# Second block of a two-block transformer: the last token tile of each feed-forward is multiplied one turn later, and the first feed-forward products stand two a step over four steps

## What is computed

```
qkv = x @ qkv_w                      # 16 heads of 16
attn = softmax(where(node_mask, q @ k.T / 4, -inf)) @ v
attn_out = attn @ proj_w + proj_b
x = x + gate_msa * modulate(layernorm(attn_out), shift_msa, scale_msa)
mlp_out = gelu(x @ fc1_w + fc1_b) @ fc2_w + fc2_b
x = x + gate_mlp * modulate(layernorm(mlp_out), shift_mlp, scale_mlp)
```

## Time and profile before

| what | value |
|---|---|
| median of 3 runs | 1455.85 us |
| profiled execution: its time, its span | 1457.03 us, 1455.2 us |
| busy share of TensorE, VectorE, ScalarE, GpSimd | 90%, 55%, 53%, 52% |
| granted TensorE clock over the span | 0.978 |
| length of turn 12 | 63.75 us |

### The profile page before, as it was taken

One profiled execution on the slowest core, in us unless ns is written; L12 is line 12 of the kernel. 1 busy time (PEld: TensorE's weight loads), 2 busy tenths in 40 slices (PEclk: granted clock), 3 DMA queues, 4 the chain that ended last, 5 costly groups with the idle time before them and its releaser, 6 DMA issues. The chain is left out here.

```text
span 1455.2 us, 24552 instructions
## 1 busy us (share of the span) xinstructions
PE 1309.6 (90%) x8789; PEld 1004.0 (69%) x8789; DVE 803.2 (55%) x2240; ACT 770.5 (53%) x1262; POOL 757.1 (52%) x939
## 2 busy tenths in 40 slices
PE   4898999999999999999999997989888898988777
PEld 3676777777777777777777775666666666665556
DVE  3766645645646656656645643464655556454452
ACT  3565665665665765665655752544544353453522
POOL 3788876776776776776776761020413222140323
PEclk9999999999999999999999998999999999999988
DMA  8432222223213213213213215353424242433100
GB/s 258 130 127 57 71 84 72 73 75 83 74 64 89 75 58 88 78 55 88 79 54 110 92 41 164 113 152 108 151 67 145 61 155 93 123 116 86 45 2 29
DMA packets 98259, 133.98 MB, mean 92 GB/s; under 512 B 16802, under 2 KB 51498, under 8 KB 98130
## 3 DMA queue, kind: packets, MB, share of 16 engines
q1 hardware_dynamic: 96850, 131.80, 30.3%
q10 hardware_dynamic: 1280, 0.53, 0.2%
HBM read 72.64 MB, written 58.75 MB: 90 GB/s over the span
## 5 line engine op out<-in xcount | busy, mean ns | idle before, releaser
L617 POOL TENSOR_SCALAR shifted<-shifted,row_max 128x512 f32<-128x512 f32 x512 | 360.6, 719 | 220.1 <-DVE row_max L1380 218.2
L1380 DVE CUSTOM_DVE_ANT_0 shifted<-score,bias 128x512 f32<-128x512 f32 x512 | 332.7, 687 | 255.4 <-PE score L855 165.6
L1091 ACT ACTIVATE probs<-turned 128x512 f32<-128x512 f32 x512 | 278.2, 596 | 211.4 <-PE turned L867 209.8
L867 PE MATMUL turned<-ident,shifted 128*128 128x128 f32 x2048 | 270.0, 275 | 6.8 <-POOL shifted L617 6.0
L867 PEld LDWEIGHTS turned<-ident,shifted 128*128 128x128 f32 x2048 | 233.6, 141 | 55.6 <-issue 26.6
L783 PE MATMUL dense<-w_down,hidden 128*128 128x256 f32 x1024 | 253.3, 383 | 0.8 <-ACT hidden L1072 0.8
L610 POOL TENSOR_SCALAR bias<-dist,scale 128x1024 f32<-128x1024 f32 x192 | 220.0, 1146 | 13.6 <-DMA down_bias<-in_L_cond_b 13.6
L855 PE MATMUL score<-k_rows,q_rows 97*128 97x512 f32 x512 | 205.2, 456 | 22.1 <-DVE row_max L1380 10.1
L783 PEld LDWEIGHTS dense<-w_down,hidden 128*128 128x128 f32 x1024 | 185.6, 191 | 32.6 <-issue 9.6
L763 PE MATMUL dense<-feat_m,w_up 128*128 128x512 f32 x768 | 188.4, 400 | 3.5 <-ACT hidden L1072 1.8
L763 PEld LDWEIGHTS dense<-feat_m,w_up 128*128 128x128 f32 x768 | 144.3, 192 | 37.1 <-ACT hidden L1072 5.3
(11 more groups left out here) (138 smaller groups left out, 1497.3 us busy)
## 6 DMA issues: line engine op xcount, KB each, us to landing
qk_rows<-qk_high SPq DMA_DIRECT2D x128, 256.0 KB
q_rows<-qk_rows SPq DMA_DIRECT2D x64, 384.0 KB
qk_rows<-qk_low SPq DMA_DIRECT2D x64, 256.0 KB
k_rows<-qk_rows SPq DMA_DIRECT2D x68, 192.0 KB
x_in_t<-in_x SPq DMA_DIRECT2D x8, 512.0 KB, 3.8
x_res<-in_x SPq DMA_DIRECT2D x8, 512.0 KB, 5.5
x_mid<-x_norm SPq DMA_DIRECT2D x8, 512.0 KB, 3.3
x_in_t<-x_mid SPq DMA_DIRECT2D x8, 512.0 KB, 3.9
```

The costliest lines, as they stand in the source:

```text
L617: ins = pool.tensor_scalar(shifted[:, u % 3, i, :], shifted[:, u % 3, i, :], -1.0, row_max[:, t % 6:t % 6 + 1], ALU.mult, ALU.add)
L867: mm = pe.transpose(turned_bank[z % 2][:, HALF * kk + P * i:HALF * kk + P * i + P], shifted[:, u % 3, i, P * kt:P * kt + P], ident[:, :])
L1091: act.activation(probs[:, u % RING, 2 * pair:2 * pair + 2, :], turned_bank[z % 2][:, :].rearrange("p (a c) -> p a c", a=2), ACT.Exp)\
L1380: dve.tensor_tensor_reduce(shifted[:, u % 3, i, :], score_bank[t % 2], bias[:, u % 2, i, :], 1.0, 3.0e38, ALU.add, ALU.min, row_max[:, t % ...
```

## The change

In turns 9 to 15 a new table `HEADS` holds. Turn 8 keeps the old one under the name `ENTER`. The last token tile of the down product of pass n-1 isn't made in turn n any more but in turn n+1, at place 7, as the piece `late`, with its eight chunks in one run; `normalize` of that pass moves from step 0 to step 3 of turn n+1, and GpSimd's `inverse_std` and `norm_offset` move with it. `t2` moves from place 7 to 9 and `qk` 3 from 8 to 10. The eight `up` pieces stand at places 13, 16, 19 and 22, two at each, instead of four at 10 and four at 13. ScalarE takes them in two groups of four, at places 16 and 22 (`HEADS_GELU`). The remaining 24 down chunks stand at places 25 to 35. In step 2 VectorE does `peaks_of` before the four `add_tile`, and no longer after them. The end after turn 15 has a list `TAIL` of its own with the late tile between `wout` and `t2`.

```diff
@@ -64,14 +64,26 @@
 
 
 
-    HEADS = {0: [("v", 3), ("t3", 0), ("t3", 1)], 1: [("t1", 0), ("t1", 1)], 2: [("wout", 0), ("wout", 1)],
+
+    ENTER = {0: [("v", 3), ("t3", 0), ("t3", 1)], 1: [("t1", 0), ("t1", 1)], 2: [("wout", 0), ("wout", 1)],
              3: [("wout", 2), ("wout", 3), ("qk", 0)], 5: [("qk", 1)],
              6: [("qk", 2)], 7: [("t2", 0), ("t2", 1)], 8: [("qk", 3)],
              10: [("up", 0), ("up", 1), ("up", 2), ("up", 3)], 13: [("up", 4), ("up", 5), ("up", 6), ("up", 7)],
              19: [("down", 0)], 23: [("down", 1)], 28: [("down", 2)], 35: [("down", 3)]}
     HEAD_STEPS = H // 2 + 4
-    HEADS_DOWN = {16: (0, 4), 17: (4, 6), 19: (6, 9), 20: (9, 11), 22: (11, 14), 23: (14, 16), 25: (16, 19),
+    ENTER_DOWN = {16: (0, 4), 17: (4, 6), 19: (6, 9), 20: (9, 11), 22: (11, 14), 23: (14, 16), 25: (16, 19),
                   26: (19, 21), 28: (21, 24), 29: (24, 25), 31: (25, 28), 34: (28, 29), 35: (29, 32)}
+
+    HEADS = {0: [("v", 3), ("t3", 0), ("t3", 1)], 1: [("t1", 0), ("t1", 1)], 2: [("wout", 0), ("wout", 1)],
+             3: [("wout", 2), ("wout", 3)], 4: [("qk", 0)], 5: [("qk", 1)], 6: [("qk", 2)], 7: [("late", TT - 1)],
+             9: [("t2", 0), ("t2", 1)], 10: [("qk", 3)], 13: [("up", 0), ("up", 1)], 16: [("up", 2), ("up", 3)],
+             19: [("up", 4), ("up", 5)], 22: [("up", 6), ("up", 7)], 28: [("down", 0)], 31: [("down", 1)],
+             35: [("down", 2)]}
+    HEADS_DOWN = {25: (0, 6), 26: (6, 7), 28: (7, 12), 29: (12, 14), 31: (14, 19), 34: (19, 22), 35: (22, 24)}
+    LATE_AT = 7
+    TAIL = [("t3", 0), ("t3", 1), ("wout", 0), ("wout", 1), ("wout", 2), ("wout", 3), ("late", TT - 1), ("t2", 0),
+            ("t2", 1)] + [("up", c) for c in range(FCH)] + [("down", t) for t in range(TT)]
+    HEADS_GELU = {16: (13, 16), 22: (19, 22)}
 
     ANY = {0: [("v", 0), ("v", 1)], 1: [("t3", 0), ("t3", 1)], 2: [("v", 2), ("v", 3)], 3: [("t1", 0), ("t1", 1)],
            4: [("wout", 0)], 5: [("wout", 1)], 6: [("wout", 2)], 7: [("wout", 3)], 9: [("qk", 0)],
...
@@ -92,28 +104,35 @@
     def bias_by_act(u):
         return u % 4 == 3
 
-    def pass_of(piece, n):
+    def of_turn(piece, n):
+
+        if piece[0] == "late":
+            return (("down", piece[1]), n - 2) if n - 2 >= B else None
         m = n - 1 if piece[0] in BACK else n + 1 if piece[0] in FRONT else n
-        return m if 0 <= m < N else None
+        return (piece, m) if 0 <= m < N else None
+
+    def pieces(table, k, n):
+        found = [of_turn(p, n) for p in table.get(k, [])]
+        return [x for x in found if x is not None]
 
     def listed(table, n):
-        return [(p, pass_of(p, n)) for k in sorted(table) for p in table[k] if pass_of(p, n) is not None]
+        return [x for k in sorted(table) for x in pieces(table, k, n)]
+
+    def tail():
+        return [of_turn(p, N) for p in TAIL]
 
 
     PLACE = []
     for second in (HEADS, ANY):
         order = listed(FIRST, -1)
         for n in range(N):
-            order += listed(FIRST if n < B else second, n)
-        order += listed(second, N)
+            order += listed(FIRST if n < B else ENTER if n == B and second is HEADS else second, n)
+        order += tail() if second is HEADS else listed(second, N)
         PLACE.append({x: i for i, x in enumerate(order)})
     chosen = {"any": 0}
 
     def place(piece, n):
         return PLACE[chosen["any"]][piece, n]
-
-    def pieces(table, k, n):
-        return [(p, pass_of(p, n)) for p in table.get(k, []) if pass_of(p, n) is not None]
...
@@ -699,6 +718,9 @@
                 else:
                     add_shift(n - 1, 0)
                     inverse_std(n - 1, 0)
+                    if n - 2 >= B:
+                        inverse_std(n - 2, 1)
+                        norm_offset(n - 2)
 
                     piece_ready(pool, ("up", 0), n - 1)
                     add_shift(n - 1, 1)
@@ -707,9 +729,6 @@
                 if n + 1 < N:
                     mask(n + 1)
                     value_mask(n + 1)
-                if n > B:
-                    inverse_std(n - 1, 1)
-                    norm_offset(n - 1)
 
             def turn(n):
                 if short(n):
...
@@ -974,25 +995,28 @@
 
             def turn(n):
                 if short(n):
+                    table, down = (ENTER, ENTER_DOWN) if n == B else (HEADS, HEADS_DOWN)
                     for p in range(HEAD_STEPS):
                         attended = p >= 5 and p % 2 == 1
                         if 2 <= p < 2 + H // 2:
                             pair_scores_of(n, p - 2)
                         for k in range(3 * p, 3 * p + 2):
-                            for piece, m in pieces(HEADS, k, n):
+                            for piece, m in pieces(table, k, n):
                                 dense(piece, m)
-                            if k in HEADS_DOWN:
-                                down_chunks(n - 1, *HEADS_DOWN[k])
+                            if k in down:
+                                down_chunks(n - 1, *down[k])
+                            if k == LATE_AT and n - 2 >= B:
+                                down_chunks(n - 2, FCH * (TT - 1), FCH * TT)
                         if attended:
                             attend_heads(n, (p - 5) // 2)
                         if 2 <= p < 2 + H // 2:
                             turn_peaks(n, p - 2)
                         if 3 <= p < 3 + H // 2:
                             turned_scores_of(n, p - 3)
-                        for piece, m in pieces(HEADS, 3 * p + 2, n):
+                        for piece, m in pieces(table, 3 * p + 2, n):
                             dense(piece, m)
-                        if 3 * p + 2 in HEADS_DOWN:
-                            down_chunks(n - 1, *HEADS_DOWN[3 * p + 2])
+                        if 3 * p + 2 in down:
+                            down_chunks(n - 1, *down[3 * p + 2])
                         if attended:
                             heads_to_tokens(n, (p - 5) // 2)
                     return
...
@@ -1015,8 +1039,10 @@
                         to_tokens(n, gq)
 
             def epilogue():
-                for piece, m in listed(ANY if chosen["any"] else HEADS, N):
+                for piece, m in listed(ANY, N) if chosen["any"] else tail():
                     dense(piece, m)
+                    if piece[0] == "down" and m == N - 2:
...
@@ -1145,12 +1171,14 @@
 
             def turn(n):
                 if short(n):
+                    table, gelus = (ENTER, {}) if n == B else (HEADS, HEADS_GELU)
+                    later = [k for group in gelus.values() for k in group]
                     for p in range(HEAD_STEPS):
                         for k in range(3 * p, 3 * p + 2):
-                            for piece, m in pieces(HEADS, k, n):
-                                dense(piece, m)
-                        if p == 0 and n - 2 >= B:
-                            normalize(n - 2)
+
+                            for x in gelus.get(k, () if k in later else (k,)):
+                                for piece, m in pieces(table, x, n):
+                                    dense(piece, m)
                         if p >= 5 and p % 2 == 1:
                             take_heads_out(n, (p - 5) // 2)
                         if 2 <= p < 2 + H // 2:
@@ -1158,7 +1186,9 @@
                         if 3 <= p < 3 + H // 2:
                             for a in range(2):
                                 head_exp(n, 2 * (p - 3) + a)
-                        for piece, m in pieces(HEADS, 3 * p + 2, n):
+                        if p == 3 and n - 2 >= B:
+                            normalize(n - 2)
+                        for piece, m in pieces(table, 3 * p + 2, n):
                             dense(piece, m)
                         if n == B and p == 6:
                             take_high(w_out, raw_out[1], "wout_loaded", "out_high", 2)
@@ -1186,9 +1216,9 @@
                     take_high(w_up, raw_up[1], "wup_loaded", "up_high", 2)
 
             def epilogue():
-                for piece, m in listed(ANY if chosen["any"] else HEADS, N):
+                for piece, m in listed(ANY, N) if chosen["any"] else tail():
                     dense(piece, m)
-                    if piece == ("t3", DC - 1) and short(N - 1):
+                    if piece == ("t2", DC - 1) and short(N - 1):
                         normalize(N - 2)
 
             run(act, prologue, turn, epilogue)
...
@@ -1490,22 +1520,22 @@
 
             def turn(n):
                 if short(n):
+                    table = ENTER if n == B else HEADS
                     for p in range(HEAD_STEPS):
-                        for piece, m in pieces(HEADS, 3 * p, n):
+                        for piece, m in pieces(table, 3 * p, n):
                             dense(piece, m)
-                        if p == 2:
-                            if n == B:
-                                first_norm("norm", 1, n - 1)
-                            else:
```

(19 more changed lines are left out.)

## The result

The changed kernel takes 1468.67 us (median of 6 runs, 1463.77 to 1471.45), the kernel before 1455.59 in the same rounds. The ratio is 1.0079, 95% interval 1.0055 to 1.0103: slower, by 11.5 us by the ratio (the medians differ by 13.1). The profiled execution has a span of 1467.8 us against 1455.2.

The account below looks back on a forecast made before the run. TensorE bounds a turn: some 54 us of products, 7.6 of waits, plus clock loss. 63.8 + 1.0 + 3.8 - 4.1 + 1.8 + 1.0 = 67.3 us a turn; together +15.4 on 1457.0, median 1471 us, range 1449 to 1485.

Parts of the forecast that it names:

- case A: The sum as forecast: TensorE's waits change place and become longer, 1460 to 1483 us; chance 0.50.
- Steps 2 and 3: TensorE waits 2.5 us before the second pair's scores and 1.5 before the second turn_peaks; net +1.0 us a turn.
- The two groups of gelus: TensorE waits 1.9 us for ScalarE's gelus before up products in steps 4 and 7; +3.8 us a turn.
- What steps 4 to 11 and the edge give back: Shorter waits for split peaks, attend_heads and t3 in steps 4 to 11 and at the turn's edge; -4.1 us a turn.
- The transfers of peaks: Turned scores wait for transfers taking 4.7 us: 1.3 in step 4, 0.8 in step 6; +1.8 us net a turn.
- The clock: TensorE's clock falls in steps 2 and 3 nearly every turn, elsewhere one in three; +1.0 us a turn, bounds 0 and 4.
- The turn: A typical turn sums to 67.3 us, 2.4 more than the mean of 64.9 over turns 10 to 14.
- Turn 9 and the end: Turn 9 grows by 3.4 us, turn 15 by 1, and the end after it shrinks by 1.
- Rival C: Transfers land in time, the clock costs nothing; turn 64.5 us, perhaps 63.0 by shorter products; 1446 to 1453 us; chance 0.23.

Follow-up runs that it names:

- e1_peaks_before_late: Changed kernel, but in step 2 of turns 9 to 15 VectorE does the first pair's take_peaks ahead of the late tile's work: 1462.58 us, ratio 1.0032.
- e2_gelu_own_place: Changed kernel, but ScalarE takes each pair of up pieces at its own place, not in two groups of four: 1447.89 us, ratio 0.9926.
- e5_store_later: Changed kernel, but in turns 10 to 15 SyncE's queue loads the next pass's first two row groups before result store and residual and modulation loads: 1460.92 us, ratio 1.0007.
- e9_filled_wait: Changed kernel with 8 useless products of 512 columns in TensorE's wait before the second pair's scores, turns 9 to 15: 1472.15 us, ratio 1.0098.
- e7_own_place_peaks_first: Changed kernel with each up pair taken by ScalarE at its own place and the first pair's take_peaks ahead of VectorE's late-tile work: 1436.83 us, ratio 0.9856.

## Why the prediction was right, and where it wasn't

The forecast was 1471 us in 1449 to 1485, case A; measured are 1468.67. By its own steps:

- **Steps 2 and 3**: forecast waits of 2.5 and 1.5 us; turn 12 has 2.38 and 1.72. That VectorE's order is the cause of the first is shown by `e1_peaks_before_late`, which halves it by an edit on VectorE alone; no run tried the second.
- **The two groups of gelus**: forecast 1.9 us twice, 3.8 a turn; measured 1.72 and 1.65 in turn 12, and 2.8 a turn over the five (14.2 us in nine waits), so this term was 1.0 too large. Shown as the cause from both sides: without groups the changed kernel gains 1.5% (0.9926 against 1.0079), the up part alone 1.0% (0.9974 against 1.0079). 3.8 us in seven turns had been 1.8%. That a table load is 1.28 us with nothing behind it holds in all rows; the second experiment has four more a turn, 5.0 us of busy ScalarE, in a turn that is 4 us shorter.
- **What steps 4 to 11 and the edge give back**: forecast 4.1 us a turn. The waits of attend_heads are gone (7.6 us in five turns), split peaks wait once a turn, and t3's is 0.53 and not 0.91.
- **The transfers of peaks**: 1.3 + 0.8 = 2.1 us of waits a turn were forecast, 1.8 after what later waits absorb; measured are 2.3. The split was not right. Step 4 was to wait 1.3 us and waited in one turn of five; step 6 was to wait 0.8 and waits 1.1 to 3.3 us, 2.0 in the mean. `e5_store_later` shows that the order in which the stored result and the two loads are issued makes step 6's. The section of the Trainium skill that the prediction cites for 2.0 us (DMA: Bandwidth & Descriptors, "Anatomy of one DMA") gives it for DMAs that GpSimd issues. These are issued on ScalarE's queue, and as little as 2.0 us was seen only where there was no other traffic.
- **The clock**: 1.0 us a turn was set for it. As a cost of slower products the size is near: TensorE is busy 0.6 us a turn more than in the five turns before, 0.9 more than in the turn 12 that the sum starts from. What was wrong is that it was added to the wait of 1.3 us in step 4. The two aren't independent: the slow products of step 4 stand where TensorE would wait for a transfer. `e9_filled_wait` and the rows of `e1_peaks_before_late` both show it, and it is why step 4's own wait is missing. What the falls elsewhere cost stays open, as no run removed them.
- **The turn**: 67.35 us against 67.3 is in part luck. Four of the five turns have a mean of 66.5, and turn 13 with 70.7 lifts it. The gelus' term was 1.0 too large and the transfers' 0.5 too small against its 1.8; the sum holds because misses of both signs make up for each other.
- **Turn 9 and the end**: forecast +3.4 and 0 (turn 15 and the end together); measured +2.2 and -0.8.
- **Rival C** (transfers land in time, faster than before) fell: with the transfers of step 6 in time (`e5_store_later`) the kernel is even with the one before, not below it. It set 2.8 us a turn for transfers and clock together; that run's turns are 1.7 shorter (65.6 us), half of it in waits and half in TensorE's busy time. Its 1.5 us of hidden products weren't there.

One thing the prediction has as a small term recurs in the experiments. In turns 10 to 14 TensorE is busy 284.0 us in the changed kernel, 274.8 in `e1_peaks_before_late`, 275.9 in `e2_gelu_own_place`, 272.6 in `e7_own_place_peaks_first`, with the same products, and the clock over all runs of these kernels is 0.9765, 0.980, 0.979 and 0.981 in the mean. So an edit that takes a wait away may also gain by faster products, and what a wait is worth can't be read from its own length alone. `e9_filled_wait` has 0.980 too and gained nothing, so a higher clock isn't a gain by itself.

## What to carry to other kernels

Where an engine works through a table in a fixed order, the place of a piece on the product's engine is only half of the move: look at what it puts in front of the small operation for which the next product waits, and put that operation first (0.5 to 0.7% here, in three pairs of kernels). Saving table loads by holding evictions back costs the engine that needs the banks; count the banks before grouping, and compare the chain up to the first eviction with the work that covers it. Slow products and a wait behind them may cover each other, so before both are added in a forecast, look whether the one ends before the other. Edits are worth trying in pairs: the edit on VectorE gave 0.5% alone and 0.7% with the gelus at their places, which these intervals don't tell apart, while the profiles show that the two gains are made up differently.

## What wasn't expected of the hardware

An 8 KB transfer could be used 2.0 us after its issue where the queues moved next to nothing (4 GB/s in the stretch of the earlier trace rows), while in the changed kernel, wherever TensorE waited for one, 4.1 to 7.5 us lay between the issue and the products. In step 6 of turn 12 these were 5.4 us, with 304 GB/s moved in the stretch; with another order of SyncE's queue under 4.0 sufficed, with 116 GB/s. And a granted clock of 1.2 GHz for 3.4 us, which made twelve products 1.6 us slower in step 4, cost at most some tenths of a microsecond there, because a transfer was still under way: without the fall, in `e9_filled_wait` and `e1_peaks_before_late`, TensorE waited 1.2 and 1.3 us for it in this turn.
